# Row-group products in two self-attention stages, and a reordered capped-score stage

## The reference, cut to what matters

```python
# L1_attn: 8 heads of 32, keys and values from a latent of 64
q = (x @ Wq.T); kv_latent = x @ Wkv_down.T
k = kv_latent @ Wk_up.T;  v = kv_latent @ Wv_up.T
attn = softmax(einsum(q, k) / sqrt(32));  x += einsum(attn, v) @ Wo.T
# L2_attn: 16 query heads of 8, 4 key/value heads, capped scores
q = rope(rms_norm(x @ w_q)); k = rope(rms_norm(x @ w_k)); v = x @ w_v     # k, v repeated 4 times
scores = tanh(einsum(q, k) / sqrt(8) / 50) * 50, causal
x += einsum(softmax(scores), v) @ w_o
```

## Time and profile before

| | us |
|---|---|
| median of 3 runs | 6953.03 |
| lowest, highest | 6949.58, 6967.59 |
| the profiled execution | 6960.73 |
| its span | 6958.9 |

### The profile page before, as it was taken

How to read it: one execution, slowest core, us unless ns; L and a number is a source line. 1 busy time by engine, 2 the same in 40 slices (tenths; PEclk the granted TensorE clock), 3 DMA queues, 4 the chain that set the end, 5 groups by cost and what they waited for, 6 DMA issues and landing times.

```text
span 6958.9 us, 164805 instructions
## 1 busy us (share of the span) xinstructions
PE 5892.8 (85%) x54018; PEld 4629.8 (67%) x54018; DVE 3846.9 (55%) x12136; ACT 2804.6 (40%) x6611; POOL 1777.1 (26%) x2870
## 2 busy tenths in 40 slices
PE   6999998788689989888888998666679988878888
PEld 5777776777457767666666776654457777866665
DVE  5666664444346656544444665554446669964444
ACT  2444441111334442254554554224445542235555
POOL 3555551000023333100001444540014433310000
PEclk9999998999679999999998998777779988789999
DMA  3000000000000000000000110000001100000000
GB/s 128 18 18 17 18 17 3 0 0 0 0 22 29 28 22 0 0 0 0 0 0 19 33 33 16 0 0 0 0 19 33 33 16 0 0 0 0 0 0 12
DMA packets 43766, 93.46 MB, mean 13 GB/s; under 512 B 7696, under 2 KB 28560, under 8 KB 42640
## 3 DMA queue, kind: packets, MB, share of 16 engines
q1 hardware_dynamic: 43664, 92.09, 4.2%
HBM read 88.92 MB, written 3.15 MB: 13 GB/s over the span
## 4 chain that ended last, share of the span: by engine, by line
issue 43%; PE 43%; DVE 8%; ACT 3%; POOL 1%; DVEq 0%; DMA 0%; POOLq 0%; SPq 0%; ACTq 0%
PE psum_banks L548 5%; PE psum_banks L553 4%; PE psum_banks L613 3%; PE psum_banks L1597 3%; PE psum_banks L657 3%; PE psum_banks L664 3%; PE psum_banks L617 2%; PE psum_banks L1573 2%; PE psum_banks L1074 2%; PE psum_banks L1632 2%; PE psum_banks L1064 1%; DVE scratch L1800 1%; PE psum_banks L1062 1%; PE psum_banks L1615 1%; DVE scratch L1346 1%
## 5 line engine op out<-in xcount | busy, mean ns | idle before, releaser
L2269 PE MATMUL psum_banks<-w_L_ffn_up,x_normed_T 128*128 128x352 f32 (+3 forms) x2112 | 890.8, 546 | 97.2 <-DVE x_normed_T L2411 63.6
L263 POOL TENSOR_TENSOR ln_vareps<-ln_meanvar,ln_eps 128x1 f32<-128x1 f32 x165 | 44.6, 270 | 2795.8 <-DVE ln_meanvar L258 2795.8
L780 DVE TENSOR_REDUCE scratch<-psum_banks 128x2 f32<-128x514 f32 x768 | 531.4, 692 | 409.0 <-PE psum_banks L548 405.0
L699 ACT ACTIVATE scratch<-psum_banks 128x512 f32<-128x512 f32 x768 | 458.5, 597 | 489.0 <-PE psum_banks L558 483.5
L2307 ACT ACTIVATE scratch<-psum_banks 128x176 f32<-128x176 f32 (+3 forms) x1120 | 398.6, 371 | 623.2 <-PE psum_banks L2269 535.3
L553 PE MATMUL psum_banks<-scratch 32*128 32x128 f32 x6144 | 637.9, 309 | 8.1 <-ACT scratch L699 6.1
L548 PE MATMUL psum_banks<-scratch 32*128 32x257 f32 x3072 | 574.2, 440 | 50.6 <-DVE scratch L781 50.6
L2269 PEld LDWEIGHTS psum_banks<-w_L_ffn_up,x_normed_T 128*128 128x128 f32 x2112 | 420.2, 224 | 233.6 <-issue 113.5
L2247 PEld LDWEIGHTS psum_banks<-consts,scratch 128*128 128x128 f32 x2144 | 276.6, 152 | 441.2 <-issue 275.0
L2255 PE MATMUL psum_banks<-w_L_ffn_down,scratch 128*128 128x128 f32 x4096 | 556.0, 282 | 10.4 <-ACT scratch L2298 10.4
L2451 DVE SCALAR_TENSOR_TENSOR scratch<-scratch,psum_banks 128x176 f32<-128x176 f32 (+2 forms) x704 | 257.8, 374 | 529.9 <-ACT scratch L2307 463.3
(11 more groups left out here) (428 smaller groups left out, 14211.1 us busy)
## 6 DMA issues: line engine op xcount, KB each, us to landing
scratch<-in_ctx SPq DMA_DIRECT2D x99, 514.0 KB, 3.5
scratch<-in_ctx_rows SPq DMA_DIRECT2D x130, 128.0 KB, 2.0
w_L_ffn_up<-in_L_ffn_up SPq DMA_DIRECT2D x1, 2992.0 KB, 10.1
w_L_ffn_down<-in_L_ffn_down SPq DMA_DIRECT2D x1, 2112.0 KB, 12.2
w_L_ffn_up<-in_L_ffn_up SPq DMA_DIRECT2D x1, 2080.0 KB, 8.1
x_tokens<-in_x SPq DMA_DIRECT2D x1, 2048.0 KB, 8.2
scratch<-last_values SPq DMA_DIRECT2D x128, 8.0 KB
out<-x_tokens SPq DMA_DIRECT2D x1, 2048.0 KB, 6.3
```

The lines of the kernel that those rows point to most:

```text
L699: act.activation(pT[:, b % 2, 2 * h:2 * h + 2].rearrange("p t c q -> p t (c q)"), W, ACT.Exp).then_inc(exp_ready.sem, 1)
L780: dve.tensor_reduce(parts[:, r.t.odd, 2 * h:2 * h + 2, 0, b], S, X_AXIS, ALU.max, negate=True)
L2269: pe.matmul(U[g % 3][:, 0:fw * halves], k.xnT[:, :], up[:, c0:c0 + fw * halves], start=True, stop=True).then_inc(sg["up_written"].sem, 1)
```

## The change

**Products of 32 rows.** In both stages the weighted values are now one product for each batch and group of four heads (`value_rows`): only the 32 rows of that batch, with 128 columns of weights, against 128 columns of values in L1 and 32 in L2. The output of batches 0 and 1 lies in one bank, that of 2 and 3 in the other (`two_banks`). A first half does batches 0 and 2 in turn, a second half 1 and 3, after a semaphore that the first half has ended. The scores of L2 are made in the same way, a product for each batch and key head (`score_rows`), of 32 rows and 32 columns. So `vm`, `kbd` and the POOL work on them are gone. In L1 ACT copies keys and values from PSUM in two instructions instead of one, the values behind the exponential.

**Order of L2.** DVE rotates first and multiplies by the root afterwards (`over_roots`); ACT makes the squares (a Square in `take_qkv`); DVE repeats the four value heads with a copy; `heads` on DVE and PE stands before the mask and the transposes of the tile behind; the residual is a round later; one round more is written out ahead of the loop and behind it.

```diff
+        two_banks = [k.psum[:, n:n + 2, :].rearrange("p o c -> p (o c)").rearrange("p (u c) -> p u c", u=4) for n in (0, 3)]
+        D, O, SUM = k.bank[0] if kind == "L1" else two_banks[0][:, :, 0:P], two_banks[1], two_banks[1][:, 0, P:P + 16]
+    plan = Plan(2, TILES - 4, TILES + 2, 2, -3) if kind == "L2" else Plan(1, TILES - 3, TILES + 1, 2, -3)
...
+    halves = {0: (0, 2), 1: (1, 3)}
...
             if kind == "L2":
-                if r.coming:
-                    pool.wait_ge(rotated.sem, rotated.at(t, 1))
-                    values(t, s["kvx"][:, P:2 * P])
-                    pool.wait_ge(mid_read.sem, mid_read.at(t, 1))
-                    pool.wait_ge(scores_written.sem, scores_written.at(r.t, 1))
-                    rows_by_head(pool, s["kbd"], s["qkT"][:, P:2 * P], k.c("quad")).then_inc(spread.sem, 1)
...
+        def score_rows(t, half):
+            for b in range(NB):
+                for g in halves[half]:
+                    rows, keys = slice(32 * g, 32 * g + 32), slice(32 * b, 32 * b + 32)
+                    mm = pe.matmul(D[:, g, keys], s["qbd"][rows, 0, b * P:(b + 1) * P], s["qkT"][rows, P + 32 * b:P + 32 * b + 32],
+                                   start=True, stop=True, skip_group_check=True)
+            return mm
+
+        def other_scores(t):
+            pe.wait_ge(scores_begun.sem, scores_begun.at(t, 1))
+            score_rows(t, 1).then_inc(scores_written.sem, 1)
...
+        def value_rows(t, half):
+            for n in range(nt):
+                cols = slice(n * 4 * hd, (n + 1) * 4 * hd)
+                for b in halves[half]:
+                    rows = slice(32 * b, 32 * b + 32)
+                    mm = pe.matmul(O[:, b, cols], s["pT"][rows, n * P:(n + 1) * P], s["vals"][rows, t.odd, cols], start=True,
+                                   stop=True, skip_group_check=True)
+            return mm
+
+        def other_values(t):
+            pe.wait_ge(values_begun.sem, values_begun.at(t, 1))
+            mm = value_rows(t, 1)
...
         def values(t):
             pe.wait_ge(turned_read.sem, turned_read.at(t, 1))
...
             for n in range(nt):
-                left, vm = s["pT"][:, n * P:(n + 1) * P], s["vm"][:, t.odd, :]
-                if kind == "L1":
-                    mm = pe.matmul(O[n][:, :], left, vm[:, n * 512:(n + 1) * 512], start=True, stop=True)
...
             elif kind == "L2":
                 act.wait_ge(mid_written.sem, mid_written.at(t + -2, 1))
+                act.wait_ge(ms_ready.sem, ms_ready.at(t + -1, 1))
+                act.wait_ge(vm_ready.sem, vm_ready.at(t + -2, 1))
+                act.activation(s["sq"], A[:, 0:160], ACT.Square)
                 act.activation(s["qkv"][:, t.odd, :], A[:, 0:192], ACT.Copy).then_inc(qkv_read.sem, 1)
...
+        def take_values(t):
+            act.wait_ge(pv_done.sem, pv_done.at(t + -2, 1))
+            act.activation(s["vals"][:, t.odd, :], MID[:, 256:512], ACT.Copy).then_inc(mid_read.sem, 1)
...
+        def over_roots(r):
+
+            t = r.t + 1
+            qkv = s["qkv"][:, t.odd, :]
+            q, kx = qkv[:, 0:P].rearrange("p (h d) -> p h d", d=8), qkv[:, P:160].rearrange("p (t d) -> p t d", d=8)
+            dve.wait_ge(rms_ready.sem, rms_ready.at(t, 1))
+            dve.wait_ge(mid_written.sem, mid_written.at(r.t, 1))
+            dve.tensor_tensor(q, q, bc(s["r"][:, 0:16], 2, 8), ALU.mult)
```

More of the change, by code:

```diff
@@ L889, in chain_steps @@
         if kind == "L2":
-            return (["heads", "cos", "sin", "low", "high"] * has.coming + ["squares", "ms"] * has.after
-                    + ["rr", "w"] * has.turned + ["stats"] * has.third)
+            return (["cos", "sin", "low", "high"] * has.coming + ["stats"] * has.third + ["rr", "w"] * has.turned
+                    + ["ms"] * has.after)
         return (["E"] * has.own + ["rr", "w"] * has.turned + ["R", "RE", "max", "nm"] * has.own + ["stats"] * has.third)
@@ L970, in one @@
                     values(t, s["qkvT"][:, 2 * P:3 * P])
-            if r.third:
+            if kind != "L2" and r.third:
                 normal(r.t + 3)
@@ L1034, in scores @@
                     cols = slice(b * P, (b + 1) * P)
[L1035 to L1045, removed]
+                    pe.matmul(D[:, cols], s["qbd"][:, 0, cols], s["kbd"][:, 0, cols], start=True, stop=False,
+                              skip_group_check=True)
+                    pe.matmul(D[:, cols], s["abd"][:, cols], s["group"], start=False, stop=False, skip_group_check=True)
+                    pe.matmul(D[:, cols], s["qbd"][:, 1, cols], s["kbd"][:, 1, cols], start=False, stop=True,
+                              skip_group_check=True)
+                    mm = pe.matmul(E[:, cols], s["rest"][:, cols], s["kbd"][:, 2, cols], start=True, stop=True,
+                                   skip_group_check=True)
             mm.then_inc(scores_written.sem, 1)
@@ L1053, in turn @@
             mm.then_inc(turned_written.sem, 1)
+        def value_rows(t, half):
[9 more added lines that the diff above has]
+            mm = value_rows(t, 1)
+            if kind == "L2":
+                for n in range(nt):
+                    mm = pe.matmul(SUM[:, 4 * n:4 * n + 4], s["pT"][:, n * P:(n + 1) * P], k.c("quad"), start=True, stop=True,
+                                   skip_group_check=True)
+            mm.then_inc(pv_done.sem, 1)
@@ L1059, in values @@
             for n in range(nt):
-                left, vm = s["pT"][:, n * P:(n + 1) * P], s["vm"][:, t.odd, :]
-                if kind == "L1":
-                    mm = pe.matmul(O[n][:, :], left, vm[:, n * 512:(n + 1) * 512], start=True, stop=True)
[L1063 to L1066, removed]
+                left = s["pT"][:, n * P:(n + 1) * P]
@@ L1067, in values @@
+                pe.matmul(batches_first(O[0])[:, :, n, :], left, batches_first(s["vm"][:, t.odd, :])[:, :, n, :], start=True,
+                          stop=True, skip_group_check=True)
+                mm = pe.matmul(SUM[:, 4 * n:4 * n + 4], left, k.c("quad"), start=True, stop=True, skip_group_check=True)
             mm.then_inc(pv_done.sem, 1)
@@ L1094, in one @@
                 turn_x(r.t + 2)
+            if kind != "L3" and r.turned:
+                other_values(r.t + -1)
             if kind == "L1" and r.own:
@@ L1106, in one @@
                 heads(r.t + -1)
+            if kind == "L2" and r.own:
+                turn(r.t)
             if kind != "L3" and r.coming:
@@ L1110, in one @@
                 output(r.t + -1)
+            if kind == "L2" and r.coming:
+                other_scores(r.t + 1)
             if kind == "L3" and r.own:
@@ L1185, in one @@
                     act.activation(s["pr"][:, 0:256], s["pr"][:, 0:256], ACT.Exp).then_inc(probs_ready.sem, 1)
-            if kind == "L2" and r.after:
-                take_x(r.t + 2)
+                if r.coming:
+                    take_values(r.t + 1)
             if kind == "L2" and r.own:
                 act.wait_ge(scores_written.sem, scores_written.at(r.t, 1))
-                act.activation(s["D"], D[:, :], ACT.Tanh, scale=float(1.0 / (CAP * np.sqrt(8.0)))).then_inc(scores_read.sem, 1)
+                act.activation(s["D"].rearrange("p (t u) -> p t u", t=4), D, ACT.Tanh, scale=float(1.0 / (CAP * np.sqrt(8.0)))).then_inc(scores_read.sem, 1)
                 act.wait_ge(scores_read.sem, scores_read.at(r.t, 1))
```

105 lines of the change are left out of this document (58 added, 47 removed).

## The result

The changed kernel takes 7018.1 us (median of 4 runs, 7014.3 to 7033.0), the kernel before 6953.9 (4 runs): a ratio of 1.0093, interval 1.0072 to 1.0113. It is 64 us slower. The time lies inside the stated range of 6890 to 7030 only because that range was drawn to take in rival C; it lies outside the forecast's own range, 6930 to 7000. What came true is C, with its chance of 0.17: its term for L2 was +63 and the stage grew by 63.6, while its +10 for L1 did not come, so its 7026 is 8 us too high.

A forecast was written before the change was run, and what follows sets the result against it. L1 was taken as bound by PE, L2 by the loop through DVE, POOL, PE and ACT that waits for the root. L2 +11 and L1 +2 made 6953 + 13 = 6966 us, own range 6930 to 7000, stated range 6890 to 7030.

The forecast's parts named there:

- rival C: L2's clock stays at 0.50, PE's 13.75 us round is the bound: L2 +63, L1 +10, 7026 us; chance 0.17.
- the clock of L2: L2 loop: mean PEclk taken as 0.59, under the 0.72 of before and above 0.50, full clock 0.18 of the time.
- L2's term: L2_attn: a round of 12.1 us in place of 11.77, +0.33 x 32 = +11 us.
- The 13.75: L2 round at half clock, us, PE's alone: 64 narrow records 6.9, 27 wide ones 6.5, with the loop branch.
- the branch: L2: the loop branch at the end of a round, which takes 9.05 us to 9.15 at full clock.
- The price of narrow records at half clock: PE in L2: 0.108 us a record, taken from L2031; 64 narrow records are 6.9 us a round.
- rival D: Narrow weight loads don't overlap, 0.144 us a record: L2 round 14.2 us, +79, L1 +13, 7045 us; chance 0.04.
- the power off the path: L2: the rotation no longer waits for POOL's power; its 3.54 us is covered by score and value products, some 6.4.
- Rivals A and B: First: PE's clock holds near 1, 6858 us, chance 0.13; second: mean PEclk 0.68 to 0.75, 6915 us, chance 0.17.
- +2 forecast: L1_attn: 11 us saved by shorter values against 13 us lost to a lower clock, between -16 and +26.
- The gain of a round at full clock: L1: values in 1.4 us for 1.91, 0.5 or 0.15 by round, mean 0.35 x 32 = 11 us saved.
- The clock's share: L1: PEclk falls from 0.98 to 0.93, each round 0.4 us longer, 13 us.

## Why the prediction came out as it did

**The step that failed is the clock of L2**, "I take 0.59": it was 0.53 from 4340 to 4400 and 0.50 from there on. By the prediction's own sum for that clock, 13.75 us a round, L2's term would have been +63; the round is 13.62 to 13.7 and the stage +63.6. The term was +11. The reason given for 0.59 was that the heads, turns and transposes are wide work that stays together. It is, and with 8 wide products (16 records) more beside it the clock did rise, to 0.67; alone it was not enough. The row that pointed to 0.50 was there, the narrow stretch with PEclk 0.58, and was used only to lower the value halfway. That the total still fell into the wide range is the luck of how the range was drawn, not a sign that this step was right.

**The 13.75 fits better than its working.** Its parts are 6.9 and 6.5, and the branch was 0.10 one paragraph earlier, which makes 13.5. The narrow records cost more than taken: 64 at 0.116 are 7.4. The 27 wide ones are what is left of 13.62, 6.2, so less than the 6.5. An undersized term and an unexplained quarter of a microsecond stand against each other. One reading was off as well, though no term rests on it: L1312's 0.32 us was not alone, since POOL's L920 started with it at 4506.06 and ran for 1.21 us.

**Right in L2.** The price of narrow records at half clock (0.108 from another stage, 0.116 measured, under the 0.144 of rival D, which so fell), the count of 91, the power off the path (POOL waits 7.5 us, then works 3.9), DVE's spread at 0.69, no table load in L2. A half of narrow records took 1.85, over the 1.7 expected. POOL was busy 149 us, 124 of them with the power, not 115.

**Rivals A and B** both rested on a clock of 0.68 or more. The rule of the Trainium skill that was weighed, TensorE: Matmul & The Clock Gate, Loop structure matters more than you think (dense matmuls keep the clock), does not agree with this trace: PE is 99% busy with no idle time in front of its steps, at 0.50.

**What the prediction left out.** It counted L2's narrow records, 32 for 8 in the scores and again in the values, and never set them against what they replace: a half of 16 takes 1.92 us here, as long as all the 4 wide products of the scores (L1036), so scores and values are two times as long on PE at the same clock. What they free is POOL, and that was worth little once the rotation no longer waits for its power: with POOL's two spreads back, the new order runs three rounds from 4496.84 to 4522.89, 8.7 us each. The starts of the heads in that version:

```profile
4496.84 1.15 PE L1131 MATMUL psum_banks<-consts,scratch 128*128 128x128 f32 x8 [0.79 <-DVE scratch L1313]
...
4522.89 2.08 PE L1131 MATMUL psum_banks<-consts,scratch 128*128 128x128 f32 x8 [0.46 <-DVE scratch L1313]
```

**L1: +2 forecast, -1.5 in one pair of traces**, where the same code varies by more than that (303.3 to 306.3, once 297.8), so the term is neither borne out nor refuted. Both halves of it are there and smaller than thought. The gain of a round at full clock is 0.25, not 0.35, and a narrow record, here of 32 rows and 128 columns, costs 0.081 to 0.084, not 0.064. But the wait is another. It is not the exponential that holds the copy of x in one round of two; the copy of the values holds it in every round from 2750 to 2785 (0.21 or 0.28 us before the projection), since it waits for this round's value products. The timeline of the changed kernel:

```profile
2762.68 0.38 ACT L1192 ACTIVATE scratch<-psum_banks 128x256 f32<-128x256 f32 x1
...
2762.96 0.27 ACT L1162 ACTIVATE x_normed_T<-psum_banks 128x128 f32<-128x128 f32 x1
...
2763.29 0.71 PE L986 MATMUL psum_banks<-x_normed_T,w_L_attn_Wq 128*128 128x128 f32 x4 [0.21 <-ACT x_normed_T L1162]
```

The clock's share was 0.02 (0.99 to 0.97), where 0.05 was taken.

## What to carry to other kernels

Set the split products against the very ones that they replace. In L2 a record of 128 rows and 128 columns became four of 32 rows and 32 columns, each half as long, so PE's time for them doubled; in L1 four records of 512 columns (1.91 us) became sixteen of 128 columns (1.3 us), and PE's time fell. Where it rises, the split can only pay if what it frees is the bound. When most of a loop becomes narrow, price the loop at the lower clock first, and ask for evidence before taking anything above it. A change that joins a good reordering with a doubtful exchange of instructions should be taken apart: here one half was worth 88 us with wide products, the other cost 152 in the new order, and the good half, beside the changed L1, made the kernel 1.2% faster (6867.7 us), with mean square and power made earlier 1.6% (6834.2).

## What the runs showed of the hardware

The granted clock did not follow TensorE's busy share: in windows of 100 us it was 0.50 at 99%, 0.67 at 98% and 1.00 at 78% in the same stage, with narrow work, with 16 wide records a round added, and with wide work in short rounds. It can also differ between executions for the same code: L1_attn of the changed kernel had 0.96 in ten traces and 1.00 in one, with a stage 5.5 to 8.5 us shorter. Work added to the bounding engine can cost next to nothing: 16 wide records a round, +2 us in the stage, in one execution.
